# One GpSimd mask for four heads per attention step in a transformer layer on one Trainium2 core

## The reference

```python
def polynomial_attention(q, k, v, degree, is_causal):     # degree 4, causal
    a = jnp.einsum('bhnd,bhmd->bhnm', q, k) ** degree
    if is_causal:
        a = jnp.tril(a)
    denom = jnp.sum(a, axis=-1, keepdims=True)
    return jnp.einsum('bhnm,bhmd->bhnd', a / denom, v)
...
x = x + attn(layernorm(x))        # x: 4 sequences x 512 tokens x 512; 16 heads of 32
x = x + moe(layernorm(x))
```

## Time and profile before

| | us |
|---|---|
| median of three timed runs | 1075.78 |
| lowest and highest of them | 1074.3 and 1088.98 |
| the profiled execution | 1074.49 |
| its span, first to last instruction | 1072.7 |

### The profile page before, as it was taken

The page is one execution under the profiler, slowest core; times in us unless marked ns, Lnnn a source line. Parts: engine busy times, 40 slices in busy tenths (PEclk is TensorE's granted clock), DMA queues, the critical chain, the costliest instruction groups (busy, mean ns, idle before and its releaser), DMA issues.

```text
span 1072.7 us, 21356 instructions
## 1 busy us (share of the span) xinstructions
PE 949.1 (88%) x5818; PEld 459.0 (43%) x5819; DVE 718.1 (67%) x1635; ACT 571.4 (53%) x1044; POOL 523.3 (49%) x738
## 2 busy tenths in 40 slices
PE   7989999899899989787787899999999999979892
PEld 5443334334443435242354445454544444434440
DVE  3888976887879688749658675565666555545552
ACT  2368984888838984976254234343444443324340
POOL 0007663665526563757201014666676665646642
PEclk9999999999999999857969999999999999999996
DMA  8113334443324433943457988898999897869884
GB/s 305 82 40 118 119 119 143 152 139 136 122 99 158 158 118 128 385 153 124 157 189 247 315 314 214 215 227 209 224 223 228 198 221 200 208 155 219 194 197 68
DMA packets 76795, 193.57 MB, mean 180 GB/s; under 512 B 10048, under 2 KB 11200, under 8 KB 75456
## 3 DMA queue, kind: packets, MB, share of 16 engines
q1 hardware_dynamic: 58816, 149.57, 41.9%
q0 software_dynamic: 17920, 43.26, 20.1%
HBM read 131.71 MB, written 61.10 MB: 180 GB/s over the span
## 4 chain that ended last, share of the span: by engine, by line
PE 37%; DVE 14%; issue 12%; ACT 10%; DMA 10%; POOL 6%; POOLq 4%; DVEq 4%; ACTq 0%; SPq 0%
DMA out<-yy,sidx 9%; PE bank L786 9%; PE bank L515 8%; PE bank L589 5%; PE bank L578 4%; PE bank L807 4%; ACT arena L960 3%; POOL wr L1157 2%; POOLq L1200 2%; PE bank L530 2%; PE bank L777 1%; ACT s_p L952 1%; POOLq L1156 1%; DVE st L1271 1%; POOL s_p L1132 1%
## 5 line engine op out<-in xcount | busy, mean ns | idle before, releaser
L786 PE MATMUL bank<-arena,xgT 128*128 (+1 forms) x1152 | 284.4, 384 | 4.3 <-ACT xgT L1094 3.4
L1132 POOL TENSOR_TENSOR s_p<-s_p,c_causal 128x128 f32<-128x128 f32 x256 | 148.7, 604 | 218.0 <-DVE s_p L1512 186.9
L1087 ACT ACTIVATE hT<-bank 128x512 f16<-128x512 f16 x96 | 57.3, 597 | 289.7 <-PE bank L796 268.6
L515 PE MATMUL bank<-arena 128*128 128x512 f32 x384 | 184.2, 628 | 11.6 <-ACT arena L921 4.6
L1140 POOL TENSOR_TENSOR arena<-arena 128x768 f16<-128x768 f32 x68 | 116.6, 1714 | 95.4 <-ACT arena L864 95.0
L786 PEld LDWEIGHTS bank<-arena,xgT 128*128 128x128 f16 x1152 | 108.2, 98 | 128.0 <-issue 38.1
L1181 POOL DMA_INDIRECT out<-yy,sidx x80 | 128.5, 1606 | 37.6 <-issue 29.2
L807 PE MATMUL bank<-wd,hT 128*128 128x512 f16 x576 | 142.1, 383 | 0.7 <-ACT hT L1087 0.7
L1799 DVE TENSOR_SCALAR yy<-bank,hsc 128x512 f32<-128x512 f32 x80 | 60.0, 751 | 122.9 <-DMA out<-yy,sidx 122.9
L960 ACT ACTIVATE arena<-bank 128x512 f32<-128x512 f32 (+3 forms) x256 | 101.2, 439 | 59.3 <-PE bank L563 59.2
L515 PEld LDWEIGHTS bank<-arena 128*128 128x128 f32 x384 | 73.2, 199 | 102.9 <-issue 88.9
(11 more groups left out here) (187 smaller groups left out, 1398.1 us busy)
## 6 DMA issues: line engine op xcount, KB each, us to landing
wd<-w_scratch SPq DMA_DIRECT2D x82, 512.0 KB
arena<-w_experts SPq DMA_DIRECT2D x34, 768.0 KB, 5.9
w_scratch<-arena SPq DMA_DIRECT2D x34, 768.0 KB, 4.5
arena<-w_scratch SPq DMA_DIRECT2D x17, 1024.0 KB, 7.4
xin<-x SPq DMA_DIRECT2D x4, 1024.0 KB, 5.5
arena<-x SPq DMA_DIRECT2D x4, 1024.0 KB, 5.5
x_scratch<-arena SPq DMA_DIRECT2D x4, 1024.0 KB, 5.1
xg<-xn_scratch SPq DMA_DIRECT2D x16, 256.0 KB, 4.3
```

The costliest lines, as they stand in the source:

```text
L515: mm = pe.matmul(bk[:], xnT[:, c, m * P:m * P + P], wqkv[:, c, w * E:w * E + E], start=(c == 0), stop=(c == EC - 1))
L786: mm = pe.matmul(bank[2 + k][:], xgT[:, k, xh * EC + c, :], w, start=(c == 0 and xh + wh == 0), stop=(c == EC - 1 and xh == 1))
L1132: pool.tensor_tensor(d, d, C["causal"][:], ALU.mult).then_inc(p4_masked, 1)
```

## The change

On GpSimd the four masks of a step become one operation over all four heads: the 128 columns at the head of each of the four rows of 512, times `causal` repeated four times. It waits for the fourth powers of heads 2 and 3 alone: heads 0 and 1 come ahead of them in the same engine's order, whichever engine it is. `p4_masked` rises once a step instead of four times, and `values` on TensorE waits for it once, ahead of its first matmul, instead of once before each head's first one. The order of all queues stays the same otherwise.

```diff
                 if kb == 0 and b + g:
                     pe.wait_ge(att_done, b * NG + g)
+                pe.wait_ge(p4_masked, b * (NG * MB) + (i + 1))
                 for n in range(2):
                     for j in range(HG):
-                        if n == 0:
-                            pe.wait_ge(p4_masked, b * (NG * MB * HG) + (HG * i + j + 1))
                         r = slice(D * j, D * j + D)
...
                 for i in range(NG * MB):
-                    for j in range(HG):
-
+                    for j in (2, 3):
                         by, n = fourth_turn[b, i, j]
                         pool.wait_ge(p4_done[by], n)
-                        d = s_p4[:, i % 2, j, 0:P]
-                        pool.tensor_tensor(d, d, C["causal"][:], ALU.mult).then_inc(p4_masked, 1)
+                    d = s_p4[:, i % 2, :, 0:P]
+                    pool.tensor_tensor(d, d, C["causal"][:].unsqueeze(1).to_broadcast([P, HG, P]), ALU.mult
+                                       ).then_inc(p4_masked, 1)
                     split_lo(b, i)
```

## The result

The changed kernel took 1085.22 us (median of 20 runs, 1079.23 to 1095.85); the kernel before, timed beside it, 1076.41 (20 runs). The ratio is 1.008, 95% interval 1.0052 to 1.0107: slower by 8.8 us. The forecast was 1073 us with a range of 1066 to 1080. The change is within the 2% that the prediction gave 0.97, but the time lies outside the range and moved the other way. The profiled execution has a span of 1087.1 us, against 1072.7.

What follows compares the result with a forecast made beforehand. The prediction took TensorE as nearest its limit in the first three sequences, GpSimd as no bound. Its terms summed to 2.5 us gained, off the median 1075.78: 1073.3, so 1073 us, range 1066 to 1080.

Steps and rivals of the forecast that it cites:

- The port: VectorE and GpSimd take turns in attention; the merged mask holds 0.95 us, as long as four, returning VectorE nothing in total.
- The duration: GpSimd's merged 128x512 mask takes 1.16 us, from a line through one mask and the split; bounds 0.95 and 1.80 us.
- rival 1: The merged operation costs as much as four masks, 1.80 us; exposed steps lose 0.64 us each, total 1081; chance 0.08.
- The tie of 209.59: Step 3 in each middle sequence, mask against L1485: gain 1.1 us if won, 0.1 if lost; 1.2 counted.
- Step 3 of four: Where L1485 comes before the merged mask, the mask ends 0.1 us sooner; 0.6 in all, half counted: 0.3 us gained.
- the second halves: Second halves of the middle two sequences: masks 0.71 us later, nearly all covered; two counted at 0.25, loss 0.5 us.
- The three waits taken from TensorE: TensorE loses three waits a step, each just ahead of a later wait on the same queue; counted at nothing.
- The end of the third sequence: 403 to 413 us, GpSimd's queue being the chain: last mask ends about 410.5 instead of 411.72; gain 1.2 us.
- The last step: Last step of the last sequence: products run until 517.15 instead of 517.42 us; gain 0.3 us.
- Rival 2: The port blocks VectorE: merged mask before L1503 loses 0.6 us; sixteen uncovered steps would lose 10 us, 1083; chance 0.12.
- Rival 4: TensorE's clock, 452 to 474 us: another idle pattern could return most of 9.5 us, about 1066, or take some; chance 0.13.
- Rival 3: Last mask comes 0.71 us later with TensorE uncovered: slower by over 2%; all 64 steps 45 us, 1121; chance 0.02.

Runs made afterwards that it cites:

- e18: e15 with four masks of 128x64 in place of 128x128, columns 64 to 127 of each diagonal block left unmasked: 1069.2 us, ratio 0.9909.
- e15: Second run of e9, on one chip with e13, e14 and e16: 1075.5 us, ratio 1.001.
- e14: The changed kernel with two mask operations of two heads each in place of one of four: 1085.7 us, ratio 1.0078.
- e1: The kernel before, four masks kept, but TensorE waits once a step, for the fourth: 1083.4 us, ratio 1.0061.
- e9: The kernel before with four masks that all wait for heads 2 and 3, and one TensorE wait a step: 1076.6 us, ratio 1.0004.
- e16: The changed kernel run again, unaltered, for a comparison on one chip and a second profile: 1088.0 us, ratio 1.0117.
- e8: The kernel before run again, unaltered, for a second profile: its attention ends at 516.6 us.
- e3: The changed kernel with the weight split replaced by a memset of zeros: 1065.2 us, ratio 0.9903 to the kernel before.
- e13: The changed kernel with dummy matmuls of zeros ahead of TensorE's wait in 22 steps: 1084.4 us, ratio 1.0095 to the kernel before.
- e5: The kernel before, its four masks all waiting for heads 2 and 3, TensorE's four waits kept: 1079.0 us, ratio 1.0034.
- e4: The changed kernel with the split held behind VectorE's last operation in steps 1 and 2 of three sequences: 1078.2 us, ratio 1.0042.
- e17: The changed kernel with a GpSimd memset of 416 columns and a drain ahead of each split: 1081.6 us, ratio 1.0053.
- e2: The kernel before with the weight split replaced by a memset of zeros: 1055.8 us, ratio 0.9804.
- e6: e1 with dummy matmuls of zeros ahead of TensorE's wait in 22 steps: 1072.7 us, ratio 0.9972 to the kernel before.
- e12: The kernel before with the dummy matmuls of e6, ahead of the first of its four waits: 1072.8 us, ratio 0.9955.

## Why the prediction was wrong

**The step that failed** is the one under "The port": the merged operation holds its turn as long as four masks together, so that VectorE "gets nothing back in total, but loses it at one place", with the sum then made "with what is upstream kept as it is". It put the port's part in the merging at nothing. Measured on one chip, with the same start and the same single wait, four operations gave 1075.5 us and one gave 1088.0. Two things are wrong in the step. First, the total is kept for the masks alone (1.07 us in one piece, 4 x 0.26 in four), but not for GpSimd's queue. VectorE lets one GpSimd operation pass for each of its own, whatever its length. At 204 us the prediction saw the four L1517 between four masks and wrote "3 x 0.25 us of the waiting goes", gain 0. By its own rule nothing of the waiting should go, and it did not ask which operation stands behind the masks: the split of 1.64 us, which now got one of the freed turns. The four took 1.5 us more, not 0.75 less. Second, what is upstream doesn't stay. L524's wait for VectorE was taken as fixed at 209.41; it was the very thing that moved, to 211.40. The sentence in the description of the chip that the engines "meet only at semaphores" is too narrow for the same reason: these two also meet where one holds up the other.

**Its other terms.** *The duration.* 1.27 us against 1.16, inside the bounds of 0.95 and 1.80, so rival 1 is out. The line was drawn through two forms, an f32 mask in place and a split with an f16 output. The masks alone lie on another one: 319, 456, 728 and 1275 ns for 64, 128, 256 and 512 columns (e18, e15, e14, after) are 182 + 2.14 ns a column. The Trainium skill says this in "GPSIMD Engine Reference", section 3.1: about 2.6 cycles an element for a two-input operation, which at its clock of 1.2 GHz would be 2.17 ns a column, an estimate; the runs agree with 2.14. *The tie of 209.59,* 1.2 us in the sum: won at 211.78, but worth nothing, since TensorE was late by then. *Step 3 of four, 0.3,* and *the second halves, 0.5 lost:* not told apart.

*The three waits taken from TensorE,* put at nothing: 0.6% in e1, nothing in e9 and e15. *The end of the third sequence,* 1.2 us gained: it did not come. The sequence ended at 419.7 us, and at 421.0 in e16, against 412.4 and 416.1 in the two profiles of before. GpSimd's masks and split were 71.5% of the chain of 403 to 413 us in the one trace, but 30.6% of the same work in e8 (407 to 417 us), so the term rested on one execution. In the window 403 to 413 us of after, which by then holds earlier work, the chain is VectorE's:

```profile
by line: DVE seen L1357 21.0%; DVE rb L1312 19.8%; DVE hs L1494 12.2%; DVE rank L1314 12.2%; DVE sel L1354 11.6%; ACT arena L930 9.6%; DVEq L1311 6.0%; ACT arena L926 4.9%; issue 3.7%; DVEq L1360 0.9%; DVEq L1355 0.3%; DVEq L1313 0.3%; DVEq
```

A window's chain is followed back from the operation that ends last in it, here one of VectorE's. The line shows which operations followed one another there, L1357's among them, of which GpSimd held one for 1.4 us; it does not show that the products waited for them. Why the sequence ended later stays open. *The last step, 0.3 gained:* from its last fourth power to the last product it took 520.48 to 522.96, 2.48 us, against 2.24 before: 0.24 lost. The mask took 1.26 us, and all sixteen products came after it, at the lower clock (0.50), 1.08 us instead of the 0.58 that was put down:

```profile
521.88 0.66 PE L577 MATMUL bank<-s_p,arena 128*32 128x128 f32 x8 [3.43 <-POOL s_p L1130]
522.31 0.65 PE L577 MATMUL bank<-s_p,ones 128*32 128x128 f32 x8
```

**The rivals.** Rival 2 was the right mechanism at the wrong place: L1503 cost nothing (24.0 us in sixteen operations before, 23.1 after), but L1517 did (twelve operations in attention, 11.2 us before, 14.3 after), and L1282 (twelve, 9.4 and 12.8) and small routing operations. It was held at 0.12. Its 1083 is nearest to the result, but by luck, since it was the price of sixteen uncovered L1503. The rule that spoke for it, an exclusive lock of the port pair for a whole instruction (the Trainium skill, "SBUF — State Buffer", "Who interferes with whom"), was weighed only by the length of the lock; at 204 us the length is the same before and after, and what counts is which operations of the queue get a turn. The traces agree with the lock but not quite with its length: a mask of 1.27 us held VectorE for 1.07, a split of 1.64 for 1.45. The same section says that an operation of GpSimd that only writes does not contend, and the memset of e3 agrees. Rival 4 was open in both directions. It went against the change: 71.7 to 105.5 us at the lower level. e1 shows 6 to 7 us lost with such a rise (71.7 to 109.1 us) and four masks, e13 that in the changed kernel the clock is not what decides. Rival 3, 45 us, did not come.

**What would show it** named, for wrong, a lower busy share of TensorE in the first three sequences, and that came, 82.78 against 87.14 of 94 us. But it is no sign of lost time: e1 has it too (82.05), and its attention is level with the kernel before there. Of the signs for right, some came although the time did not: masks of up to 2.3 us, and fewer waits of TensorE for the mask, 44 instead of 99. Others missed: GpSimd was busy 49.7 us less, not 40, the waits were 56.0 us, not 35 to 50, and the third projection came 7.3 us later (3.6 against e8), not 1 to 3 sooner.

**What stays open.** The parts don't add: e1 is 0.6% slower and e5 0.3%, both together (e9, e15) not at all, though their time at the lower clock is nearly as long as e1's, and then merging costs the whole 0.8 to 1.1%. So why the single wait costs in e1 is not settled either. The split's coming forward explains the two places at 204 and 334 us, 1.5 us each. By the ratios e4 and e17 give back 4 and 3 us of the first measurement of the changed kernel (1.008), 8 and 7 of the second (1.0117), with intervals that overlap either. The other held operations are counted (35 to 60), but which of them reach the end was not shown. The distance of e3 to e2, with no split at all, suggests that the mask's own hold can be enough for a loss of that size; a kernel with the memset, the late start, the single wait and four masks would tell, and was not run.

## What to carry to other kernels

Where two engines take turns operation by operation, as VectorE and GpSimd did here, count turns and not only columns. Merging short operations saved busy time of their engine (49.7 us), but it let the long operation behind them come forward (1.5 us lost at each of two places), and it held operations of 0.17 us for over 1 us. If the engine that gains is not the bound, look at what its queue does next with the time saved, use more than one profile where a term is of 1 us, and don't take a group of waits turned into one on TensorE as free.

## What the hardware showed

- An operation of VectorE with 4 columns took 1.21 us beside a GpSimd mask, one with 16 columns up to 1.59 us beside a split, against 0.16 to 0.18 alone.
- Four VectorE operations of 0.68 us took 2.49 us alone; 3.53 with four masks of 0.45 us in GpSimd's queue and a split of 1.64 behind them; 3.28 where VectorE had started before the first mask; 5.01 with one mask or two and the split; 3.56 with one mask and a memset.
- One of these four was held for 0.12, 0.26, 0.54 and 1.07 us by a mask of 64, 128, 256 and 512 columns (e18, before, e14, after) and for 1.45 by a split of 768. That is 1.9 to 2.1 ns a column, and about 0.2 us less than the GpSimd operation takes alone.
- Dummy products of zeros ahead of a wait gave 10.7 us back in one kernel (e6 against e1, 47 us less at the lower clock), about 4 in another (e12 against before, 4 to 10 us less), and 3.5 in a third, with intervals that overlap (e13 against e16, 53 us less).
